# Two running sums for the attention probabilities on POOL, and another place for the experts' token weights

## What is computed

```python
h = layernorm(x) * (1 + ca) + sa
xq, xk, xv = h @ wq.T, h @ wk.T, h @ wv.T        # each reshaped to (16 heads, 2048, 64)
p = softmax(xq @ xk.T / 8)                       # per head, 2048 x 2048
x = x + ga * ((p @ xv) @ wo.T)
h = layernorm(x) * (1 + cb) + sb
s = sigmoid(h @ gate_w.T); the 2 experts with the largest s + bias are chosen
routed_e = h * s[e]
y = shared(h) + sum over the chosen e of s[e] * (silu(routed_e @ w1[e].T) * (routed_e @ w3[e].T)) @ w2[e].T
x = x + gb * y
```

## Time and profile before

| | |
|---|---|
| median of 3 runs | 1362.94 us (1361.97 to 1363.24) |
| the profiled execution | 1362.54 us |
| its span, from the first to the last instruction | 1360.7 us |
| granted TensorE clock, mean share of full speed | 0.995 |
| PE busy | 1338.5 us (98%) |
| POOL busy | 1188.5 us (87%) |
| DVE busy | 918.3 us (67%) |
| ACT busy | 669.5 us (49%) |

### The profile page before, as it was taken

The page is one execution under the profiler, slowest core; times in us unless marked ns, Lnnn a source line. Parts: engine busy times, 40 slices in busy tenths (PEclk is TensorE's granted clock), DMA queues, the critical chain, the costliest instruction groups (busy, mean ns, idle before and its releaser), DMA issues.

```text
span 1360.7 us, 21599 instructions
## 1 busy us (share of the span) xinstructions
PE 1338.5 (98%) x8714; PEld 699.9 (51%) x8714; DVE 918.3 (67%) x1024; ACT 669.5 (49%) x837; POOL 1188.5 (87%) x537
## 2 busy tenths in 40 slices
PE   7999999999999999999999999999999999999998
PEld 5544545454554545454544545454545545454565
DVE  5767667676767676676766676676767676746755
ACT  6454545454544545454544545554545545465331
POOL 2499999999999999999999999999999999999443
PEclk8999999999999999999999999999999999999999
DMA  7010202020010202020100102020201002003231
GB/s 203 3 45 1 47 2 47 1 47 1 22 27 1 47 1 48 1 47 1 44 4 9 39 1 48 1 48 1 47 1 27 22 1 48 1 1 63 63 99 57
DMA packets 31957, 41.51 MB, mean 31 GB/s; under 512 B 4298, under 2 KB 15186, under 8 KB 31858
## 3 DMA queue, kind: packets, MB, share of 16 engines
q1 hardware_dynamic: 31714, 40.13, 12.4%
q10 hardware_dynamic: 144, 0.00, 0.0%
HBM read 13.70 MB, written 1.11 MB: 11 GB/s over the span
## 4 chain that ended last, share of the span: by engine, by line
PE 95%; DVE 3%; ACT 1%; DMA 0%; issue 0%; SPq 0%; DVEq 0%
PE ps L1200 35%; PE ps L1123 15%; PE ps L1176 9%; PE ps L1179 9%; PE ps L1182 9%; PE ps L1100 4%; PE ps L1226 2%; PE ps L1104 2%; PE ps L442 2%; PE ps L428 2%; PE ps L1213 2%; PE ps L443 2%; DVE peak_parts L930 1%; PE ps L1188 1%; DVE ps L950 0%; DMA probs<-in_L_attn_wq_dram 0%
## 5 line engine op out<-in xcount | busy, mean ns | idle before, releaser
L857 POOL TENSOR_TENSOR acc<-acc,probs 128x1024 f32<-128x1024 f32 x448 | 1068.3, 2385 | 68.2 <-ACT probs L791 3.4
L930 DVE TENSOR_REDUCE peak_parts<-ps 128x2 f32<-128x1024 f32 x512 | 624.1, 1221 | 304.7 <-PE ps L1123 299.9
L791 ACT ACTIVATE probs<-ps 128x1024 f32<-128x1024 f32 x512 | 496.8, 1023 | 398.3 <-PE ps L1182 322.6
L1200 PE MATMUL ps<-probs,v_sb 128*64 128x512 f32 x2048 | 507.5, 606 | 0.0
L1200 PEld LDWEIGHTS ps<-probs,v_sb 128*64 128x64 f32 x2048 | 126.3, 136 | 195.9 <-issue 166.5
L1176 PE MATMUL ps<-q_hi,d_swap_hi 64*128 64x512 f32 x512 | 201.5, 394 | 0.0
L1176 PE MATMUL ps<-q_hi,d_hi 64*128 64x512 f32 x512 | 201.4, 393 | 0.0
L1179 PE MATMUL ps<-q_lo,d_hi 64*128 64x512 f32 x512 | 200.3, 391 | 0.0
L1182 PE MATMUL ps<-q_hi,d_swap_lo 64*128 64x512 f32 x512 | 200.2, 391 | 0.0
L1182 PE MATMUL ps<-q_hi,d_lo 64*128 64x512 f32 x512 | 200.1, 391 | 0.0
L1179 PE MATMUL ps<-q_lo,d_swap_hi 64*128 64x512 f32 x512 | 200.0, 391 | 0.0
(11 more groups left out here) (147 smaller groups left out, 1084.4 us busy)
## 6 DMA issues: line engine op xcount, KB each, us to landing
k_swap_hi<-k_hi SPq DMA_DIRECT2D x64, 128.0 KB, 2.3
d_swap_hi<-d_hi SPq DMA_DIRECT2D x64, 128.0 KB, 2.3
d_swap_lo<-d_lo SPq DMA_DIRECT2D x64, 128.0 KB, 2.3
token_weights<-weights_dram SPq DMA_DIRECT2D x32, 256.0 KB, 3.2
probs<-in_L_ffn_w_dram SPq DMA_DIRECT2D x2, 512.0 KB, 5.5
shifts<-shift_sb SPq DMA_DIRECT2D x64, 2.0 KB
out_dram<-probs SPq DMA_DIRECT2D x4, 256.0 KB, 3.0
x_in<-in_L_attn_x_dram SPq DMA_DIRECT2D x1, 960.0 KB, 8.8
```

Source lines behind the costliest of these rows:

```text
L791: act.activation(probs[:, kt % PROBS, :], ps[:, 2 * place:2 * place + 2, :].rearrange("p a b -> p (a b)"), ACT.Exp, scale=SCALE).then_inc( ...
L857: pool.tensor_tensor(total, total if kt > 1 else probs[:, 0, :], probs[:, kt % PROBS, :], ALU.add).then_inc(added, 1)
L930: dve.tensor_reduce(peak_parts[:, :, i // STRETCHES, i % STRETCHES], ps[:, bank:bank + 2, :], AX.X, ALU.max).then_inc(peak_free, 1)
L1200: mm = pe.matmul(ps[at:at + HEAD_DIM, PV_BANK, :], v_sb[:, p, chunk_of(kt) * HEAD_DIM:(chunk_of(kt) + 1) * HEAD_DIM], probs[:, kt % PROBS, ...
```

## The change

POOL keeps two running sums. Additions are numbered n = 1 to 15 (`ADDS`). n = 1 puts tiles 0 + 1 into the even sum (`acc[:, half, :]`), n = 2 puts tiles 2 + 3 into the odd sum (a new tile `acc_odd`, one for all units), n = 3 to 14 add tile n + 1 to the even and the odd sum by turns, each after a wait for addition n - 2 and not n - 1, and n = 15 adds the odd sum to the even one, after a wait for n = 14. `adds(kt)`, the number of the addition that frees tile `kt`, changes with it: tiles 0 and 1 are freed by addition 1, tiles 2 and 3 by addition 2, tile `kt` from 4 on by addition `kt` - 1. The count per unit stays 15. VectorE's work is the same: it takes all the peaks, as before.

The tile `token_weights` (8 x 512 float32 per partition) is gone. `token_weight[e]` is a quarter of parity 0 of `q_hi`, `q_lo`, `k_hi` and `k_swap_hi` by turns, two experts in each tile.

```diff
-        token_weights = sb("token_weights", [P, EXPERTS, BANK])
...
         acc = sb("acc", [P, 2, HALF])
+        acc_odd = sb("acc_odd", [P, HALF])
...
+        ADDS = TILES - 1
+
         def adds(kt):
-            return max(1, kt)
+            return kt // 2 + 1 if kt < 4 else kt - 1
...
-        token_weight = [token_weights[:, e, :] for e in range(EXPERTS)]
+        token_weight = [buf[:, 0, i * BANK:(i + 1) * BANK].bitcast(F32) for buf in (q_hi, q_lo, k_hi, k_swap_hi)
+                        for i in (0, 1)]
...
-            dve.wait_ge(added, (UNITS - 1) * (TILES - 1) + 9)
+            dve.wait_ge(added, (UNITS - 1) * ADDS + adds(9))
...
-                                    act.wait_ge(added, unit * (TILES - 1) + (adds(old % TILES)
-                                                - (TILES - 1 if old < 0 else 0)))
+                                    act.wait_ge(added, unit * ADDS + (adds(old % TILES) - (ADDS if old < 0 else 0)))
...
-            def add_tile(unit, half, kt):
-
-                pool.wait_ge(exped, unit * TILES + (kt + 1))
-                total = acc[:, half, :]
-                if kt > 1:
-                    pool.wait_ge(added, unit * (TILES - 1) + (kt - 1))
-                pool.tensor_tensor(total, total if kt > 1 else probs[:, 0, :], probs[:, kt % PROBS, :],
-                                   ALU.add).then_inc(added, 1)
+            def add(unit, half, n):
+
+                even, odd = acc[:, half, :], acc_odd[:, :]
+                total = even if n % 2 == 1 else odd
+                if n == ADDS:
+
+                    pool.wait_ge(added, unit * ADDS + (n - 1))
+                    pool.tensor_tensor(even, even, odd, ALU.add).then_inc(added, 1)
+                elif n <= 2:
+
+                    kt = 2 * n - 2
+                    pool.wait_ge(exped, unit * TILES + (kt + 2))
+                    if n == 2 and unit > 0:
+
+                        pool.wait_ge(added, unit * ADDS)
+                    pool.tensor_tensor(total, probs[:, kt, :], probs[:, kt + 1, :], ALU.add).then_inc(added, 1)
+                else:
+                    kt = n + 1
+                    pool.wait_ge(exped, unit * TILES + (kt + 1))
+
+                    pool.wait_ge(added, unit * ADDS + (n - 2))
+                    pool.tensor_tensor(total, total, probs[:, kt % PROBS, :], ALU.add).then_inc(added, 1)
...
-                    for kt in range(1, TILES):
-                        add_tile(unit, half, kt)
+                    for n in range(1, ADDS + 1):
+                        add(unit, half, n)
...
-                pe.wait_ge(added, unit_done * (TILES - 1) + (TILES - 1))
+                pe.wait_ge(added, unit_done * ADDS + ADDS)
```

## The result

The changed kernel takes 1368.37 us, the median of 6 runs (1367.54 to 1369.47), against 1363.09 us of the kernel before on the same chip (6 runs, 1361.97 to 1365.14): ratio 1.0037 [1.0024, 1.005], 5.3 us slower. That is beyond the 0.2% that was called measurable and above the range's upper end of 1365.6. The profiled execution took 1367.54 us (span 1365.7, against 1360.7 before), so 5.0 us of span are to be found.

A forecast was written before the change was run, and what follows sets the result against it. TensorE, not POOL, was taken to bound the kernel. Body 0, token weights' place 0, gates +2.5 and experts -2.2 gave +0.3 us on 1362.54, so 1362.8; the forecast given was 1363.0 us, range 1361.3 to 1365.6.

The forecast's parts named there:

- Cost of the body: 0: Units in mid-kernel: POOL's denser additions delay nobody, 0 us, bounds 0 and +1 us in all.
- The turns: Last unit: VectorE's SBUF steps and POOL's additions exclude each other; L521 ends one addition later, transposes 2.5 us later.
- Additions 2.33 us apart, units unchanged, 1.9 us of room at the sum: Body: independent additions 2.33 us apart, units still 36.85 and 38.67 us, TensorE's sum keeps 1.9 us of room.
- The token weights' place, 0: Token weights' DMAs: only their target tile changes, 0 us, allowing +-0.3 us.
- The gates, +2.5: Last unit's routing: VectorE's last small step loses its turn to POOL, transposes start +2.5 us later, bounds +0 and +5.
- The experts, -2.2: Step into the experts: POOL's last addition ends earlier, about 1262.8, so VectorE isn't held before item 4; -2.2 us.
- rivals 1: Last unit: the gates are not late, L521 finds a free moment; 1362.2 us, chance 0.20.
- 2: Body: POOL becomes the bound, additions cost over 2.52 us; at 2.6 us each +37 us, 1400; chance 0.04.
- 4: Body: TensorE follows POOL after all, up to 2.5 us off each of some 30 units, 1290 us; chance 0.03.
- 5: Body: the gap between additions stays at 2.51, late sums cost +1, 1364 us; chance 0.05.
- Rival 3: Last unit: gates lose one more turn, or VectorE is held at item 4 too; +1.2 to +5, say 1365; chance 0.18.

The follow-up runs named there:

- experiment 1: Kernel before with only the token weights' new place, one running sum kept: 1362.79 us, ratio 0.9998.
- experiment 2: Changed kernel with the token weights back in a tile of their own, two running sums kept: 1367.77 us, ratio 1.0035.
- experiment 6: Changed kernel, but addition 8 of the next-to-last unit waits for addition 7 again: 1363.75 us in a single run.
- experiment 4: Kernel before plus a POOL memset ahead of the addition of tile 7 in the next-to-last unit: 1366.51 us, ratio 1.0021.
- experiment 5: Changed kernel with intermediate values of VectorE's step before L504 in PSUM in the next-to-last unit: 1363.01 us, ratio 0.9998.
- experiment 9: Kernel before with the token weights' new place and VectorE summing tiles 8 to 11 of the last unit: 1361.28 us, ratio 0.9991.
- experiment 3: Changed kernel with POOL's addition of tile 8 in the next-to-last unit held until VectorE sends shift_ln: 1367.27 us, ratio 1.0019.
- experiment 7: Changed kernel with POOL held for shift_ln in the next-to-last unit and for weights_ready at the last unit's addition 2: 1364.39 us, ratio 1.0004.

## Why the prediction was wrong

The step that failed is "Cost of the body: 0". It asked what the denser additions do to POOL's readers and to the slots, and never what they do to VectorE's SBUF steps in the body. The turns were worked out with care, but only for the gates and the experts, where the trace of before already showed a loss. Where it showed none, as at L496 and L497, the steps weren't priced.

- **Additions 2.33 us apart, units unchanged, 1.9 us of room at the sum**: right.
- **The token weights' place, 0**: right (experiment 1).
- **L496 and L497, no term**: 4.33 us where they took 0.40, +3.9 on VectorE and +3.4 on TensorE, which is the path. Before, L496 asked at 1201.78, 0.2 us before an addition's end, and L497 slipped into the gap. After, POOL is no longer behind in this stage: it waits for the exponential at L797 (1.78 us at 1200.29). L503 asks 0.34 us after POOL's start in the changed kernel (1200.29 and 1200.63) and 0.35 in experiments 2 (1200.12 and 1200.47) and 6 (1200.56 and 1200.91), so it meets nearly a whole addition each time; what ties the two together isn't shown. Experiments 2, 4, 5 and 6 show operands, phase and gap to be the three conditions.
- **TensorE's clock, no term**: +1.7 after its stand of 3.31 us and +1.5 behind the small matmuls. The first fall is in the two profiles with that stand (the changed kernel and experiment 2, 3.29 us) and in none of the ten others. The second is in profiles of one sum too (experiments 4 and 9), so it isn't shown to be a cost of the change.
- **The gates, +2.5**: the mechanism was right (2.35 us in the changed kernel, 2.31 in experiment 5 with the transposes at 1241.31) and worth 0 here, TensorE being later still. Its upper bound, +5, was exceeded in experiment 3 (5.8, of which 0.4 was there at 1200).
- **The experts, -2.2**: -0.9, since POOL's last addition ended at 1266.65 and not at 1262.8; it shifted with the exponentials that feed it.
- **The rivals**: nobody's additions became the bound, TensorE didn't follow POOL, and the gap did go, so rivals 1, 2, 4 and 5 fall. Rival 3 had the right mechanism and the right direction but looked for it one unit too late; its 1365 was 3.4 us short.

**Open.** Another +0.5 us appears near item 20 of the experts, not followed. In experiments 3, 4 and 7 the runs of one kernel spread over 3 to 5 us. In experiment 3 it isn't the clock that splits them: its mean share is 0.993 to 0.995 in the five shorter runs and 0.993 or 0.994 in the seven longer ones, and 4 us of 1363 would lower it by some 0.003 (an estimate: a mean share lower by 0.001 is 1.4 us of full speed lost). That leaves the turns, which one profile can't show. In the changed kernel the clock does go with the time: 1367.5 to 1367.9 at 0.993, 1368.9 to 1369.5 at 0.991. That the first rise of 1.7 us is the clock's doing rests on the rows' clock and timing; no run has the stand without the fall. Why the clock falls behind the small matmuls in some executions and not in others isn't shown; of the 29 runs of the kernel before that were timed beside experiments 1 to 4, 14 have a mean share of 0.992 or 0.993, against 0.995 in the profiled one.

## What to carry to other kernels

When one engine's instructions are packed without gaps, list every short step of the other engine that takes turns with it, in every stage and also where it costs nothing today, with the engine that waits behind it; price each at one whole instruction of the packed engine, and a chain of k such steps at k of them, as the two here (2.07 and 2.26 us against additions of 2.38 and 2.33). A gap that looks like waste can be the only place where such steps get in, and moving the operands to PSUM took these two steps out of the contest (0.17 us each, experiment 5). Where the packed engine holds up only the tail, taking work off it there (experiment 9) did better than running it without gaps, though its gain over the kernel before isn't clear of the noise.

## What the runs showed that was not expected

- Steps over 12 elements cost as much as the instruction that they meet: 2.07 and 2.26 us against 0.17.
- A loss can cover another: with the first place cured, the gates were 5.8 us late in the profiled execution of experiment 3, and most of its runs were no faster.
- The granted clock fell to 1.2 GHz for some 3.4 us after a stand of 3.31 us, and once more behind the matmuls of 8 columns, where the kernel before showed 1.00. The second fall came with one sum too, without a stand, and cost 1.5 us (experiment 9 against 1).
